# Set-up and first two steps of a conditional attention block in another order

## The chip, the cores and the metric

The kernel runs on one NeuronCore of a Trainium2 chip. The metric is the time of the whole kernel on the device in microseconds (us). Before the change the median of three runs is 350.76 us (348.23, 350.76, 350.86).

## The reference, cut to what matters

Sixteen batches of 256 tokens with 256 features go through one block: a normalisation scaled by a condition, attention with 16 heads of 16 features, a projection with residual, and a second conditional normalisation.

```python
h = _sln(hidden, w, ln_g, ln_b, Wg, bg, Wb, bb)     # gamma(w) * ln(hidden) + beta(w)
qkv = (h @ Wqkv.T + bqkv).reshape(B, N, num_heads, hd, 3)
energy = jnp.einsum('bhqd,bhkd->bhqk', q, k)
att = jax.nn.softmax(energy, axis=-1) / D ** 0.5
out = jnp.einsum('bhqk,bhkd->bhqd', att, v)          # heads put side by side again
h1 = (out @ Wp.T + bp) + hidden
return _sln(h1, w, ln_g, ln_b, Wg, bg, Wb, bb) + h1
```

## The kernel before, in words

**Numbers.** Everything is float32. To multiply on TensorE with enough precision, each operand is split into a high part of type `fp32r` (`hT_h`, `wqkv_h`, `qk_h`) and a low part, the difference (`hT_l`, `wqkv_l`, `qk_l`); a product is three matmuls (high by high, low by high, high by low).

**Stacks.** Per batch, q and k of each head are copied by DMA into `qst` and `kst`, where one head has its high and low parts on different partitions, so that a single contraction gives q times k. A batch has two groups of eight heads (`g` = 0, 1). For each group `send(a, g, t, low)` (L286) on SyncE's queue issues two DMAs of 128 KB: `t` is 0 for q and 1 for k, `low` is 0 for the high part and 1 for the low part. A whole group is eight DMAs. The places of `kst` that no DMA writes must be 1.0 (`ones_k`, L455, GpSimd) and those of `qst` 0 (`clear_q`, ScalarE). The sends of k wait for that fill through `kpad_ready`.

**Two passes of scores.** `scores_max(a, h)` (L1003) computes the scores of head h of batch a into the banks `sa0`, `sa1`; VectorE reduces each bank to row maxima (`maximum`, L681, the TENSOR_REDUCE of L688). After eight heads TensorE transposes the maxima (`transpose_max`, L1067), ScalarE makes the high part `m_h` (`high_max`, L505), VectorE the low part `m_l` (`low_max`, L692), and two small DMAs put both as two more rows into `qst` (`maxima`, L361, GpSimd; for batch 0 group 0 ScalarE issues them itself, L566). Then `scores(b, h)` (L1016) computes the scores less the maximum into `st0`, `st1`, and ScalarE takes the exponential (L602). A `scores_max` may run at most two heads ahead of VectorE's maxima, since there are two banks.

**Steps.** Each engine runs its own program of steps; step b has 16 slots h, one for each head. In slot h of step b TensorE computes `scores(b, h)` and `scores_max(b + 1, h)`, and between them the other work of the neighbouring batches in slots given by constants at L45 to L55: q, k and v projections, `turn_x` (L1092, transposes the normalised input of batch b + 3), `weigh` (weights times v), the output projection. Step -1 has no `scores`: only the maxima of batch 0, the k projection of batch 1 (slots 0 to 3), the v projections of batches 0 and 1 (`V_FIRST`, slots 4 to 6 and 9 to 12) and `turn_x(2)` in slot `X_FIRST` = 8.

**Order on each engine.** Every engine executes its list in order, and semaphores hold it. The order of each list is written out by hand. In step -1 the following matters:
- GpSimd: `low_full(1, 0)` (low part of batch 1's q, L415) in slot 0. In slot 5: `rstd_x(2)`, `low_full(1, 1)` (low part of batch 1's k, which gives `kl_ready` its second count), `norm_x(2)` (xn of batch 2, two instructions of L378), then `wp_l`. In slot 12 `low_h(2)`.
- TensorE, slot 8: `scores_max(0, 8)` and then `turn_x(2)`, which waits for `xn_ready`; slot 9: `scores_max(0, 9)` and `transpose_max(0, 0)`.
- ScalarE, slot `X_FIRST` + 1 = 9: `hT` of batch 2 (L584, waits for `turn_x(2)`) and `hT_h` (L503). Slot 10: `high_max(0, 0)` and the two DMAs of L569, and slot 13 `high_v(1)`.
- VectorE, slot 9: `low_max(0, 0)`, which waits for `high_max(0, 0)`, ahead of `maximum(0, 9)`.
- SyncE's queue: the sends of batch 0 (the high part of k of group 0 goes by ScalarE's queue, `high_k0`, L620), then those of batch 1, in the order that the code below shows.

In step 0, slot 1, TensorE transposes the maxima of heads 8 to 15 of batch 0 (`transpose_max(0, 1)`), ScalarE takes `high_max(0, 1)` in slot 2, VectorE `low_max(0, 1)` in the middle of slot 2, and GpSimd issues `maxima(0, 1)` in slot 3; `scores(0, 8)` waits for these.

Of the kernel before, what the change touches and what calls it, by code (L numbers as in the profile page):

```python
# [32 lines left out]
P = 128  # L33
B, N, D, H = 16, 256, 256, 16
HD = D // H
# [11 lines left out]
S_QH, S_KH, S_VH = 5, 7, 9  # L47
WARM = (10, 4, 4, 4)
V_FIRST = ((4, 5, 6, 6), (9, 10, 11, 12))
X_FIRST = 8  # L50
PIECE = 2
NSTK = 8
NX = 6
# [4 lines left out]
def cond_block(nc, x, condT, vectors, WgT, WbT, WqkvT, WpT, bp, out):  # L58
    gb_dram = nc.dram_tensor("gb_rows", (B, 2 * D), F32, kind="Internal").ap()
    with ExitStack() as ctx:  # L60
# [177 lines left out]
        def has(a):  # L238

            return 0 <= a < B  # L240

        def first(a):

            return a == 0
# [28 lines left out]
        def _(sp):  # L273
# [12 lines left out]
            def send(a, g, t, low):  # L286

                p, s = par(a), stack_in[g][par(a)]
                wait(sp, st_done, 16 * (a - 2) + HH * (g + 1))
                if a < 2 and t == 0:  # L290
                    sp.wait_ge(qpad_ready, 2 * a + g + 1)
                if a < 2 and t == 1:
                    sp.wait_ge(kpad_ready, a + 1)
                wait(sp, ((qh_ready, ql_ready), (kh_ready, kl_ready))[t][low], 1 * a + 1)
                src = (qk_h, qk_l)[low][:, p, t, g, :]
                for n in (low, low + 2) if t == 0 else (2 * low, 2 * low + 1):
                    sp.dma_start(raw((qst, kst)[t][PART_ROW[n]:P:P // HD, p, g * HH:(g + 1) * HH, :]),
                                 raw(src)).then_inc(s, 16)
# [34 lines left out]

            send(0, 0, 0, 0)
            send(0, 0, 0, 1)
            send(0, 0, 1, 1)
            for t in range(2):
                for low in range(2):
                    send(0, 1, t, low)
# [16 lines left out]
        def _(pool):  # L356
# [61 lines left out]
            def step(b):  # L418
                for h in range(H):
                    if h == 5 and has(b):  # L420

                        one, two = has(b + 3), has(b - 2)
                        if one:
                            wait(pool, v_step, 3 * (b + 3) + 3)
                            wait(pool, xn_ready, 1 * (b + 3))
                        if two:
                            wait(pool, ln2_step, 4 * (b - 2) + 3)
                            wait(pool, y_ready, 1 * (b - 2))
                        which = slice(0 if one else 1, 2 if two else 1)
                        pool.tensor_tensor(rstd[:, which], vare[:, which], minus_half[:, which],  # L430
                                           ALU.pow).then_inc(rstd_ready, 1)
                    if first(b + 1) and h == 0:
                        low_full(1, 0, ql_ready)
                    if first(b + 1) and h == 5:
                        rstd_x(2)
                        low_full(1, 1, kl_ready)
                        norm_x(2)
                        pool.wait_ge(wph_ready, 1)
                        pool.tensor_tensor(wp_l[:], wp[:], wp_h[:], ALU.subtract).then_inc(wpl_ready, 1)
                    if h == 3:  # L440
                        maxima(b, 1)
                    if h == 11 and has(b):
                        maxima(b + 1, 0)
                    if h == 6 and has(b - 2):
                        add_beta(b - 2)
                    if h == 5 and has(b + 3) and has(b):
                        norm_x(b + 3)
                    if h == 0 and has(b - 1):
                        add_bias(b - 1)
                    if h in (13, 14) and b == B - 2:  # L450
                        add_bias(b + h - 13)
                    if h == 12:
                        low_h(b + 3)
# [20 lines left out]
                o = pool.tensor_scalar(bias_cols[:, k, :], ones[:, 0:P], vecs[:, 6, k:k + 1], D ** -0.5, ALU.mult, ALU.mult)  # L474
            o.then_inc(bias_cols_ready, 1)
            pool.memset(v_st[:, :, :, :, HD:VC].rearrange("p a t h d -> p (a t h) d"), D ** 0.5).then_inc(v_ones_ready, 1)
            rstd_x(1)
            pool.wait_ge(xn_ready, 2)
            ones_k(1, 0, H).then_inc(kpad_ready, 1)
            pool.wait_ge(wvh_ready, 1)  # L480
            pool.tensor_tensor(wqkv_l[:, :, 2 * D:3 * D], wqkv[:, :, 2 * D:3 * D], wqkv_h[:, :, 2 * D:3 * D],
                               ALU.subtract).then_inc(wvl_ready, 1)
# [13 lines left out]
        def _(act):  # L496
# [55 lines left out]
            def step(b):  # L552
                for h in range(H):
                    if h == S_O1:
                        evict_out(b - 1, 1)
                    if h == S_O0:
                        evict_out(b, 0)
                    if h == S_QH and not first(b + 1):
                        high_q(b + 2)
                    if h == S_KH and not first(b + 1):  # L560
                        high_k(b + 2)
                    if h == S_MT1 + 1 and has(b):
                        high_max(b, 1, pv_ps[0])
                    if h == S_MT0 + 1 and has(b + 1):
                        high_max(b + 1, 0, pv_ps[1] if first(b + 1) else m1)
                    if h == S_MT0 + 1 and first(b + 1):  # L566
                        for r, m, ready in ((0, m_h, mh_ready), (1, m_l, ml_ready)):
                            act.wait_ge(ready, 1)
                            act.dma_start(raw(qst[MAX_ROW + r:MAX_ROW + 1 + r, 0, 0:HH, :])  # L569
                                          .rearrange("a h (t n) -> a (h t) n", t=TT),  # L570
                                          raw(m[:, 0, :])).then_inc(max_first, 16)
                    if h == S_AT + 1 and has(b - 1):
                        wait(act, attT_done, 1 * (b - 1) + 1)
                        wait(act, proj_done, 1 * (b - 2) + 1)
                        nc.scalar.activation(aT_h[:].rearrange("p k n -> p (k n)"), pv_ps[1][:],
                                             ACT.Copy).then_inc(aTh_ready, 1)
                    if h == S_VH and has(b + 1) and has(b - 1):
                        high_v(b + 1, m0)
                    if h == (X_FIRST if first(b + 1) else S_XT) + 1 and has(b + 3):
                        a = b + 3  # L580
                        wait(act, xnT_done, 1 * a + 1)
                        wait(act, hTl_ready, 1 * a)
                        for k in range(KT):
                            o = nc.scalar.activation(hT[:, k, :], m0[:, k * N:(k + 1) * N], ACT.Identity,  # L584
                                                     bias=bfull[:, k, a:a + 1], scale=gfull[:, k, a:a + 1])
                        o.then_inc(hT_ready, 1)
                    if h == (X_FIRST if first(b + 1) else S_XT) + 1:
                        high_h(b + 3)
                    if h == 4 and first(b + 1):
                        high_k(1)  # L590
                        full(1, 1, m1)
                    if h == 7 and first(b + 1):
                        high_v(0, st_ps[0])
                    if h == 13 and first(b + 1):
                        high_v(1, st_ps[1])
                    if has(b):

                        i = 16 * b + h
                        wait(act, st_done, i + 1)
                        if h % HH == 0:  # L600
                            wait(act, pv_done, 2 * (b - 1) + h // HH + 1)
                        nc.scalar.activation(p32[:, h, :], st_ps[h % 2][:], ACT.Exp).then_inc(exp_done, 1)  # L602
# [17 lines left out]
            def high_k0():  # L620

                act.wait_ge(kpad_ready, 1)
                act.wait_ge(kh_ready, 1)
                for r in PART_ROW[0:2]:
                    act.dma_start(raw(kst[r:P:P // HD, 0, 0:HH, :]),
                                  raw(qk_h[:, 0, 1, 0, :])).then_inc(stack_in[0][0], 16)

            def full(a, t, ps):

# [50 lines left out]
        def _(dve):  # L680
# [169 lines left out]
            def step(b):  # L850
# [14 lines left out]
                    (15, 0): [lambda: normalise(b, 0, 0)],  # L865
                    (15, 1): [lambda: normalise(b, 0, 1)],
                }
                if first(b + 1):
                    for slot in ((4, 0), (4, 1), (5, 0), (5, 1), (7, 1), (11, 0)):
                        del between[slot]  # L870
                    between[(9, 0)] = [lambda: low_max(0, 0)]
# [41 lines left out]
            low_qk(0, 0, m0, qh_ready, ql_ready)  # L913
            low_qk(0, 1, m1, kh_ready, kl_ready)
            norm1(1, 3)
            for stage in range(3):
                norm1(2, stage)
            h_direct(1)
            low_h_direct(1)
            set_up_rows()  # L920

            steps(step)
# [44 lines left out]
        def _(pe):  # L967
# [278 lines left out]
            def step(b):  # L1246
                for h in range(H):
# [18 lines left out]
                        out_by_token(b - 1, 1)  # L1266
                    if h == S_OT0:
                        out_by_token(b, 0)
                    if h == S_MT1 and has(b):
                        wait(pe, att_ready, 2 * (b - 1) + 1)  # L1270
                        if first(b):
                            pe.wait_ge(gbrow_ready, 1)
                        transpose_max(b, 1, pv_ps[0])
# [103 lines left out]
```

## Time and profile before

| | |
|---|---|
| runs | 348.23, 350.76, 350.86 us, median 350.76 us |
| profiled execution | 349.5 us on the device; 347.7 us from its first to its last instruction |
| TensorE (PE) busy | 334.0 us, 96% |
| VectorE (DVE) busy | 297.0 us, 85% |
| ScalarE (ACT) busy | 242.8 us, 70% |
| GpSimd (POOL) busy | 159.0 us, 46% |
| mean granted TensorE clock | 0.990 of full speed |

The page cuts the span into 40 equal slices of 8.7 us. A digit is the busy share of a slice in tenths:

```profile
PE   8886989999999999999999999999999999999993
PEclk9997899999999999999999999999999999999999
```

TensorE is nearly always busy except in the first five slices and the last; the clock granted to it is below full speed in the fourth and fifth, from about 26 to 43 us.

### The profile page before, as it was taken

To read this page: it belongs to the slowest core of one execution; us is meant where nothing else is said; L and a number is where in the kernel's file an instruction comes from. 1 tells how busy PE (TensorE), PEld (TensorE's weight loads), DVE (VectorE), ACT (ScalarE), POOL (GpSimd) and SP (SyncE) were. 2 spreads that over 40 slices of the span, in tenths; PEclk is the share of its full clock that TensorE was granted. 3 is DMA by queue.
4 is the path that set the end of the run, shared out by engine and by line. 5 is a ranking of instruction groups with operands and counts; after the bars stand their busy time and mean duration, and the time that the engine had idled before them with its cause. 6 is when DMAs were issued, how large, how long until landed. Compare 5 with 4: busy or idle time off the path is not lost.

```text
span 347.7 us, 8982 instructions
## 1 busy us (share of the span) xinstructions
PE 334.0 (96%) x3173; PEld 288.6 (83%) x3173; DVE 297.0 (85%) x728; ACT 242.8 (70%) x476; POOL 159.0 (46%) x187
## 2 busy tenths in 40 slices
PE   8886989999999999999999999999999999999993
PEld 4675968889898888888898888888898888888773
DVE  4874877789898989989898989989898988998684
ACT  7762686868678686868687686868687686766740
POOL 5476261525464462726454462726454453225330
PEclk9997899999999999999999999999999999999999
DMA  8487245544555465565545565656546454652011
GB/s 239 128 202 204 58 123 151 150 134 129 161 131 158 135 180 155 136 173 139 157 133 156 134 176 153 141 154 160 156 135 154 106 170 124 168 147 75 18 60 60
DMA packets 47705, 48.87 MB, mean 141 GB/s; under 512 B 6287, under 2 KB 41374, under 8 KB 47662
## 3 DMA queue, kind: packets, MB, share of 16 engines
q1 hardware_dynamic: 44782, 47.00, 49.3%
q0 software_dynamic: 1984, 0.51, 0.9%
q10 hardware_dynamic: 896, 0.80, 0.8%
q8 instruction: 25, 0.41, 0.5%
q14 instruction: 18, 0.15, 0.1%
HBM read 9.99 MB, written 4.23 MB: 41 GB/s over the span
## 4 chain that ended last, share of the span: by engine, by line
PE 86%; DVE 5%; ACT 2%; DMA 2%; POOL 2%; issue 2%; SPq 0%; DVEq 0%; POOLq 0%; ACTq 0%
PE m L969 24%; PE st L969 19%; PE sa L969 18%; PE pv L969 17%; PE pv L1058 4%; PE pv L1139 2%; PE m L1098 2%; DMA wqkv<-WqkvT_dram 2%; DVE mx L688 1%; DVE qk_l L723 1%; POOL qk_l L415 1%; POOL xn L378 1%; PE pv L1072 1%; PE m L1072 1%; ACT qk_h L522 0%
## 5 line engine op out<-in xcount | busy, mean ns | idle before, releaser
L688 DVE TENSOR_REDUCE mx<-sa 128x2 f32<-128x512 f32 x256 | 171.6, 683 | 30.1 <-PE sa L969 29.0
L602 ACT ACTIVATE p<-st 128x512 f32<-128x512 f32 x240 | 140.9, 598 | 38.0 <-PE st L969 33.9
L969 PE MATMUL sa<-kst,qst 126*128 126x256 f32 x512 | 106.5, 290 | 1.6 <-DVE mx L688 1.1
L969 PE MATMUL st<-qst,kst 128*128 128x256 f32 x496 | 104.0, 292 | 0.7 <-DMA qst<-m_l 0.5
L969 PEld LDWEIGHTS st<-qst,kst 128*128 128x128 f32 x496 | 75.1, 188 | 14.3 <-issue 12.8
L969 PEld LDWEIGHTS sa<-kst,qst 126*128 126x128 f32 x512 | 80.0, 193 | 3.8 <-DVE mx L688 2.1
L369 POOL DMA_DIRECT2D qst<-m_h x31 | 17.6, 566 | 117.0 <-DVE m_l L697 117.0
L969 PE MATMUL pv<-p,v_st 128*32 128x256 f32 x1008 | 61.0, 382 | 0.0
L969 PEld LDWEIGHTS pv<-p,v_st 128*32 128x32 f32 x1008 | 29.5, 109 | 21.0 <-ACT p L602 1.8
L969 PE MATMUL m<-hT_h,wqkv_h 128*128 128x256 f32 x128 | 36.8, 300 | 1.4 <-issue 0.8
L378 POOL TENSOR_SCALAR xn<-xa,mv,rstd 128x256 f32<-128x256 f32 x28 | 34.2, 1227 | 1.4
L969 PE MATMUL m<-hT_h,wqkv_l 128*128 128x256 f32 x128 | 34.4, 280 | 0.4 <-DVE wqkv_l L909 0.4
L969 PE MATMUL m<-hT_l,wqkv_h 128*128 128x256 f32 x128 | 34.2, 279 | 0.0
L430 POOL TENSOR_TENSOR rstd<-vare,minus_half 128x4 f32<-128x4 f32 (+1 forms) x15 | 14.2, 947 | 40.4 <-DVE vare L745 36.3
L550 ACT ACTIVATE oT<-pv 128x512 f32<-128x512 f32 x29 | 17.2, 594 | 21.6 <-PE pv L969 21.6
L723 DVE SCALAR_TENSOR_TENSOR qk_l<-m,vecs,qk_h 128x256 fp32r<-128x256 f32 x60 | 25.9, 473 | 0.6 <-ACT qk_h L522 0.6
L969 PEld LDWEIGHTS m<-hT_h,wqkv_h 128*128 128x128 f32 x128 | 23.5, 189 | 2.3 <-ACT wqkv_h L642 1.2
L969 PEld LDWEIGHTS m<-hT_h,wqkv_l 128*128 128x128 f32 x128 | 23.6, 190 | 0.6 <-DVE wqkv_l L909 0.6
L969 PEld LDWEIGHTS m<-hT_l,wqkv_h 128*128 128x128 f32 x128 | 23.4, 187 | 0.0
L396 POOL TENSOR_TENSOR h1b<-h,gb 128x512 f32<-128x512 f32 x15 | 19.3, 1289 | 6.9 <-DVE h L784 6.9
L387 POOL TENSOR_TENSOR xa<-xa,bias_b 128x512 f32<-128x512 f32 x16 | 20.6, 1292 | 0.0
L410 POOL TENSOR_TENSOR hT_l<-hT,hT_h 128x512 fp32r<-128x512 f32 x14 | 18.0, 1289 | 4.0 <-ACT hT_h L503 4.0
(149 smaller groups left out, 568.3 us busy)
## 6 DMA issues: line engine op xcount, KB each, us to landing
qst<-qk_h SPq DMA_DIRECT2D x64, 128.0 KB, 2.4
qst<-qk_l SPq DMA_DIRECT2D x64, 128.0 KB, 2.5
kst<-qk_l SPq DMA_DIRECT2D x64, 128.0 KB, 2.7
kst<-qk_h SPq DMA_DIRECT2D x62, 128.0 KB, 2.4
xa<-x_dram SPq DMA_DIRECT2D x16, 256.0 KB, 3.0
gb<-gb_rows SPq DMA_DIRECT2D x16, 256.0 KB, 3.9
out_dram<-y SPq DMA_DIRECT2D x15, 256.0 KB, 3.4
wqkv<-WqkvT_dram SPq DMA_DIRECT2D x1, 512.0 KB, 5.8
```

What stands on the lines that cost most here:

```text
L369: pool.dma_start(raw(qst[MAX_ROW + r:MAX_ROW + 1 + r, p, g * HH:(g + 1) * HH, :]) .rearrange("a h (t n) -> a (h t) n", t=TT), raw(m[:, g, ...
L378: o = pool.tensor_scalar(xn[:, t, :], xbuf(a)[:, t, :], mv[:, t, 0:1], rstd[:, 0, t:t + 1], ALU.subtract, ALU.mult)
L387: pool.tensor_tensor(xbuf(a), xbuf(a), bias_b[:].rearrange("p (a n) -> p a n", a=1).broadcast_to([P, TT, D]), ALU.add).then_inc(xdb_ready, 1)
L396: pool.tensor_tensor(h1b[:], h1[:], gb[:, par(a), D:2 * D].rearrange("p (a n) -> p a n", a=1) .broadcast_to([P, TT, D]), ALU.add).then_inc ...
L410: pool.tensor_tensor(hT_l[:, par(a)], hT[:], hT_h[:, par(a)], ALU.subtract).then_inc(hTl_ready, 1)
L430: pool.tensor_tensor(rstd[:, which], vare[:, which], minus_half[:, which], ALU.pow).then_inc(rstd_ready, 1)
L550: nc.scalar.activation(oT[:, g, :], pv_ps[g][:], ACT.Copy).then_inc(oT_ready, 1)
L602: nc.scalar.activation(p32[:, h, :], st_ps[h % 2][:], ACT.Exp).then_inc(exp_done, 1)
L688: dve.tensor_reduce(mx[:, par(a), h // HH, (h % HH) * TT:(h % HH + 1) * TT], sa_ps[h % 2][:].rearrange("p (t n) -> p t n", t=TT), AX.X, AL ...
L723: o = dve.scalar_tensor_tensor(out=qk_l[:, par(a), t, g, :], in0=ps[:, g * N:(g + 1) * N], scalar=vecs[:, 4 + t, g:g + 1], in1=qk_h[:, par ...
L969: return nc.tensor.matmul(o, l, r, start=start, stop=stop)
L1058: o = nc.tensor.transpose(pv_ps[g][:, t * N + c * P:t * N + (c + 1) * P], oT[:, g, c * N + t * P:c * N + (t + 1) * P], ident[:])
```

## The change

Six edits, all in the set-up and in steps -1 and 0. `X_FIRST` goes from 8 to 10, on TensorE and (one slot later) on ScalarE. On GpSimd xn of batch 2 comes ahead of the low part of batch 1's k, and the fill of batch 1's `kst` is cut in two, the first eight heads ahead of `rstd_x(1)`. The two sends of the low part of k of batch 0, group 0 move from SyncE's queue to ScalarE's. In step 0 the transpose of the second maxima and the `high_max` and `low_max` behind it come one slot sooner. On VectorE the small statistics of batch 2 (`norm1(2, 1)` and `norm1(2, 2)`) come behind `h_direct(1)` and `low_h_direct(1)`.

```diff
-X_FIRST = 8
+X_FIRST = 10
@@ sync: the sends ahead of the steps
             send(0, 0, 0, 0)
             send(0, 0, 0, 1)
-            send(0, 0, 1, 1)
@@ gpsimd, step
                     if first(b + 1) and h == 0:
                         low_full(1, 0, ql_ready)
+                        rstd_x(2)
+                        norm_x(2)
                     if first(b + 1) and h == 5:
-                        rstd_x(2)
                         low_full(1, 1, kl_ready)
-                        norm_x(2)
@@ gpsimd, set-up
+            ones_k(1, 0, HH)
             rstd_x(1)
             pool.wait_ge(xn_ready, 2)
-            ones_k(1, 0, H).then_inc(kpad_ready, 1)
+            ones_k(1, HH, H).then_inc(kpad_ready, 1)
@@ scalar, step
-                    if h == S_MT1 + 1 and has(b):
+                    if h == (0 if first(b) else S_MT1) + 1 and has(b):
                         high_max(b, 1, pv_ps[0])
@@ scalar, high_k0
                 for r in PART_ROW[0:2]:
                     act.dma_start(raw(kst[r:P:P // HD, 0, 0:HH, :]),
                                   raw(qk_h[:, 0, 1, 0, :])).then_inc(stack_in[0][0], 16)
+                act.wait_ge(kl_ready, 1)
+                for r in PART_ROW[2:4]:
+                    act.dma_start(raw(kst[r:P:P // HD, 0, 0:HH, :]),
+                                  raw(qk_l[:, 0, 1, 0, :])).then_inc(stack_in[0][0], 16)
@@ vector, step
+                if first(b):
+                    between[(1, 1)] = between.pop((2, 1))
@@ vector, set-up
             norm1(1, 3)
-            for stage in range(3):
-                norm1(2, stage)
+            norm1(2, 0)
             h_direct(1)
             low_h_direct(1)
+            norm1(2, 1)
+            norm1(2, 2)
             set_up_rows()
@@ tensor, step
-                    if h == S_MT1 and has(b):
+                    if h == (0 if first(b) else S_MT1) and has(b):
                         wait(pe, att_ready, 2 * (b - 1) + 1)
                         if first(b):
                             pe.wait_ge(gbrow_ready, 1)
                         transpose_max(b, 1, pv_ps[0])
```

## Rows read from the trace of the kernel before

**Rows 1.** Windows: start:end, length, busy us per engine, clock, DMA share, GB/s.
```profile
20.00:50.00 30.00, 25.05 (x189) 22.19 (x187) 20.68 (x41) 16.98 (x36) 15.87 (x17) 0.89 0.57 149
50.00:340.00 290.00, 289.32 (x2876) 253.06 (x2876) 259.65 (x633) 211.44 (x423) 130.62 (x143) 1.00 0.51 138
```
**Rows 2.** Chain of waits, first 60 us: start us, us, what it went through.
```profile
25.10 1.30 POOL qk_l L415
26.39 2.43 POOL xn L378 x2
28.96 0.64 PE m L1098 x4
...
44.82 0.80 DVE qk_l L723 x2
...
45.66 0.33 PE m L1072
```
**Rows 3.** Windows, same columns, the stretch at the lower clock.
```profile
30.00:36.60 6.60, 5.55 (x24) 4.95 (x24) 4.06 (x7) 2.03 (x5) 1.33 (x2) 0.50 0.74 190
```
**Rows 4.** Timeline of VectorE, 21 to 40 us; in brackets idle before, and releaser.
```profile
21.21 4.55 DVE L688 TENSOR_REDUCE mx<-sa 128x2 f32<-128x512 f32 x7 [1.52 <-PE sa L969]
26.01 1.29 DVE L688 TENSOR_REDUCE mx<-sa 128x2 f32<-128x512 f32 x2 [0.25 <-PE sa L969]
31.50 0.28 DVE L697 SCALAR_TENSOR_TENSOR m_l<-pv,m_h 16x128 fp32r<-16x128 f32 x1 [4.20 <-ACT m_h L512]
...
33.26 0.69 DVE L688 TENSOR_REDUCE mx<-sa 128x2 f32<-128x512 f32 x1 [0.29 <-PE sa L969]
34.33 0.69 DVE L688 TENSOR_REDUCE mx<-sa 128x2 f32<-128x512 f32 x1 [0.37 <-PE sa L969]
35.39 1.29 DVE L688 TENSOR_REDUCE mx<-sa 128x2 f32<-128x512 f32 x2 [0.38 <-PE sa L969]
36.90 2.01 DVE L688 TENSOR_REDUCE mx<-sa 128x2 f32<-128x512 f32 x3 [0.22 <-PE sa L969]
39.16 0.69 DVE L688 TENSOR_REDUCE mx<-sa 128x2 f32<-128x512 f32 x1 [0.25 <-PE sa L969]
39.76 0.27 DVE L697 SCALAR_TENSOR_TENSOR m_l<-pv,m_h 16x128 fp32r<-16x128 f32 x1
```
**Rows 5.** Chain of waits, first 60 us: TensorE's pieces at full clock.
```profile
37.10 0.24 PE sa L969 x2
37.34 0.36 PE m L969 x3
...
46.76 0.44 PE m L1098 x4
```
**Rows 6.** Timeline of GpSimd: set-up and step -1.
```profile
13.30 0.72 POOL L464 TENSOR_TENSOR rstd<-vare,minus_half 128x2 f32<-128x2 f32 x1 [2.11 <-DVE vare L745]
16.24 3.81 POOL L458 MEMSET kst<- 128x512 f32 x8 [2.22 <-DVE xn L750]
...
23.09 0.71 POOL L464 TENSOR_TENSOR rstd<-vare,minus_half 128x2 f32<-128x2 f32 x1
```
**Rows 7.** Timeline of SyncE's queue: batch 1's last k send of group 0.
```profile
27.82 1.20 SPq L297 DMA_DIRECT2D kst<-qk_l  x2
```
**Rows 8.** Page, DMA issues: count, KB each, median us from issue to landing.
```profile
kst<-qk_l SPq DMA_DIRECT2D x64, 128.0 KB, 2.7
```
**Rows 9.** Timeline of ScalarE and its queue, around the first sends.
```profile
14.71 1.35 ACTq L625 DMA_DIRECT2D kst<-qk_h  x2
17.12 1.25 ACT L616 ACTIVATE hT_h<-st,bfull,gfull 128x256 fp32r<-128x256 f32 x2 [2.49 <-PE st L1098]
```
**Rows 10.** Windows, same columns, while batch 0 is stacked.
```profile
16.00:21.00 5.00, 3.93 (x25) 2.77 (x24) 3.47 (x11) 2.72 (x7) 4.76 (x9) 1.00 1.11 250
```
**Rows 11.** Waits of TensorE, 20 to 50 us: us in total, times, longest.
```profile
PE st L969 <- DMA qst<-m_l: 0.5, 1, 0.5
PE sa L969 <- DMA kst<-qk_l: 0.5, 1, 0.5
```

## The prediction
> **What bounds the kernel now.** I read the windows first. From 50 to 340 us TensorE is busy 289.3 of 290.0 us at full clock; from 20 to 50 us it is busy 25.1 of 30.0 us and its mean granted clock is 0.89 [rows 1]. So whatever moves the moment at which TensorE takes over moves the end by the same amount, and only the front can give anything. The second view, the chain of waits [rows 2], shows what set that moment: GpSimd's low part of batch 1's k (25.10), then xn of batch 2 (26.39, 2.43 us), then `turn_x(2)` at 28.96. TensorE's list is in order, so slot 8 of step -1 stood idle about 2.6 us until xn was there, with `scores_max(0, 9)` behind it. The clock fell behind this idle time: from 30.0 to 36.6 us it is 0.50, the 1.2 GHz level [rows 3].
>
> The third view, VectorE's timeline, gives the bill [rows 4]. The sixteen maxima of batch 0 run from 21.21 on. Behind the ninth, VectorE sits 4.20 us idle: `low_max(0, 0)` stands ahead of `maximum(0, 9)` and waits for ScalarE's `m_h`, which stood behind `hT` and `hT_h` of batch 2, which waited for `turn_x(2)`. Then come gaps of 0.29, 0.37, 0.38, 0.22 and 0.25 us, in which VectorE waits for a half-clocked TensorE. With the 0.25 ahead of the eighth maximum the idle time from 21.21 to 39.16 is 5.96 us. From 39.16 VectorE has no gap up to 45.62, where its low part of batch 2's k releases TensorE (chain: 44.82 + 0.80, then `transpose_max(1, 0)` at 45.66 [rows 2]). From there TensorE is the bound. So 21 to 45.6 us is a VectorE stretch with 5.96 us of holes, and the question is how many holes the change closes.
>
> **xn of batch 2 first, X_FIRST 10.** GpSimd ends `low_full(1, 0)` at about 23.1, its rstd takes 0.71 (from 23.09 [rows 6]), xn 2.43 more [rows 2]: xn is there at 26.2, or 26.5 with the 0.25 us delay worked out below, not at 28.8. TensorE reaches `turn_x(2)` now behind `scores_max(0, 10)`, which waits for the maximum of head 8, at 27.3 (26.01 + 1.29 [rows 4]). So xn has nearly 1 us in hand and the idle 2.6 us goes. On ScalarE `high_max(0, 0)` stands now ahead of `hT`. The maxima of heads 0 to 7 end at 26.65, the transpose takes until about 27.2 (0.3), `m_h` 0.25: `low_max` starts at 27.5, and the 4.20 us hole becomes 0.2. Behind it run heads 9 to 15 at 0.66 us each (4.55 / 7 = 0.65 [rows 4]). TensorE's share per slot is 0.24 for two scores and 0.36 for three projections, 0.60 us [rows 5], just under VectorE's pace. Only slot 10 has 0.44 more for `turn_x` [rows 5], 1.04 in all, which I cost at a gap of 0.25. The maximum of head 15 ends at 27.7 + 7 x 0.66 + 0.25 = 32.6 us. Before, it was the first of the three from 36.90, thus at 37.57.
>
> **The maxima of step 0 one slot sooner.** TensorE now wants the maximum of head 15 in slot 0, ahead of q's first quarter (0.36) and `scores(0, 1)` (0.24), which hid this wait before. Transpose at 32.6, then 0.11 + 0.36 + 0.24, then `scores_max(1, 1)` and its drain (0.5): `maximum(1, 1)` can start at 33.85, while `maximum(1, 0)` ended at 33.25. That is a new hole of 0.6 us on VectorE, the price of this edit. In return `m_l` is ready at 34.75 by this count. Before it was 39.76 + 0.27 = 40.03 [rows 4] and `scores(0, 8)` waited 0.5 us for its landing [rows 11]. TensorE would wait less there, but VectorE sets the pace in that stretch, so I count nothing.
>
> Left of the 5.96 us are 0.25 + 0.2 + 0.25 + 0.65 (the 0.6, rounded up): 1.35. **Saved: 4.6 us** on VectorE; counted through single starts I get 4.5 (`maximum(1, 3)` ends at 36.1, not 40.6). I take 4.5.
>
> **The low part of batch 1's k behind xn.** It ends at about 26.5 + 1.3 = 27.8 us. SyncE's queue sent it at 27.82 before [rows 7], since the queue was then the slower one. Now the queue is 1.3 us ahead by the moved send, and waits for this: all it gained is spent here, and the eight DMAs of group 1 behind it leave when they did (1.3 us for each pair, the last about 34.3). The send lands at about 28.5 + 2.7 [rows 8] = 31.2; `scores_max(1, 0)` wants it at 32.0. Margin 0.8 us, cost nothing; if GpSimd were 1 us later, this wait would be the next bound, us for us. Group 1 is landed by 37 and wanted at about 39.
>
> **k's low rows on ScalarE's queue.** Its two issues of the high part ran 14.71 to 16.06. Two more take as much, 1.35 us, up to 17.4, and `hT_h` of batch 1 started at 17.12 [rows 9]: 0.3 us later. The second half of it had waited for VectorE, which now comes to `h_direct(1)` 0.1 us sooner; net 0.25 us later for `project_second`, for q of batch 1 and so for GpSimd's `low_full(1, 0)` (used above). Does the first score come sooner? It waited 0.5 us for these rows [rows 11]. The DMA engines carry 250 GB/s with a share of 1.11 from 16 to 21 us [rows 10], that is, they have no room, and an earlier issue only changes who waits. Bounds: 0.25 us sooner (the projection ahead of it then sets the start) and 0.6 us later (one more 128 KB transfer at 250 GB/s is 0.5 us, in the same engines). I take 0. The Trainium skill, DMA: Bandwidth & Descriptors, Issuing engines are not separate DMA queues, says that DMAs from all issuers interleave on the same 16 engines and that a second issuer saves only the time to issue. By that rule the move would give 0 and the sum stays; a count by issue time alone would have given 0.25 us.
>
> **GpSimd's fills.** Eight fills take 3.81 us [rows 6]; four of them, 1.9 us, now stand in the 2.11 us that GpSimd idled ahead of rstd [rows 6]. That hides them by 0.2 us; behind rstd there was another idle of 2.22 us, so that a slip costs nothing either. The other four end at 18.15 instead of 20.0, and v's low part starts sooner; nobody waits for it before slot 4. Cost and gain 0. VectorE's `norm1` pieces (0.4 us) move into the idle 1.52 us ahead of the first maximum [rows 4]: 0.
>
> **The sum.** 349.5 (profiled execution) - 4.5 = 345.0 us. This execution lies 1.3 us below the median of the runs, and the mean of all four is 349.8; against that the sum is 345.3. I predict **345.4 us**.
>
> **Rivals.**
> 1. *The clock falls all the same* (0.12). In slots 13 to 15 TensorE has only 0.24 us of work in 0.66 us. Before, the clock fell behind an idle 2.6 us and stayed at 1.2 GHz for 6.6 us although TensorE was busy 5.55 of them [rows 3]. If it falls at about 32 us, the 6.6 us behind it do half their work: 3.3 us back, saving 1.2, 348.6 us. Against it: the shares in these slots are above those of the empty 2.6 us. The Trainium skill, TensorE: Matmul & The Clock Gate, Part 1, has it that the default state is throttled and that activity releases it. The fall behind the idle stretch agrees; by that rule the thin slots are the place to fear.
> 2. *Late landings* (0.15). The first score 0.6 us later and batch 1's first stack 1 us later than I think, both from full DMA engines: saving 4.5 - 0.6 - 0.9 = 3.0, 346.8 us.
> 3. *Given back at the hand-over* (0.06). The gain on VectorE meets something of TensorE's own between 33 and 45 us (it was busy nearly all that time); then only the idle 2.6 us comes off: 347.2 us.
> 4. *Slower* (0.05). SyncE's queue: batch 1's last k send and eight DMAs behind it hang on GpSimd's `low_full(1, 1)`, now behind xn. From 32.0 us each us of lateness is lost at `scores_max(1, 0)`; from 36.5 on the change loses. xn and the low part would have to take 8 us instead of 3.7, or rstd wait for VectorE until 27: priced at 6.5 us late, 345.4 + 6.5 = 351.9, past 354.3 with 9 us. Nothing in the rows points there.
>
> **Chances.** Forecast 0.62. About 1% (3.5 us) is what a measurement of this kernel can tell, so faster means under 347.25 us. From the forecast 0.56 falls there, from rival 2 0.09: faster 0.65. Rivals 1 and 3, half of rival 2 and the forecast's edge: within 1% 0.31. Slower 0.04. The range goes from 343.6 (all holes but 0.25 closed, 5.7 us, from 349.5, less scatter of 0.2) to 348.9 (rival 1 and scatter).
>
> **What would show it.** Right: no wait of `turn_x(2)` for xn; VectorE's wait for `m_h` of batch 0 under 0.5 us; clock 1.00 from 20 to 50 us; `transpose_max(1, 0)` near 41.2; a hole near 0.6 us ahead of `maximum(1, 1)`; the first score at 20.4 to 21.2; from there to the end the same length as before. Wrong: clock 0.50 anywhere from 28 to 40 us; `scores_max(1, 0)` waiting for a `kst` landing; SyncE's queue still sending group 1 after 36 us.

## The result and the profile after

The changed kernel takes 345.31 us (median of four runs, 344.94 to 347.6); the kernel before 349.72 us (median of four, 348.23 to 350.86). The ratio is 0.9898 with a 95% interval of 0.9861 to 0.9935. The profiled execution took 345.56 us, its span is 343.8 us. Predicted were 345.4 us.

First the windows of the kernel after, to be read against [rows 1] (columns as there).

```profile
20.00:50.00 30.00, 27.46 (x218) 23.79 (x217) 25.69 (x50) 20.65 (x43) 16.69 (x17) 1.00 0.59 152
50.00:340.00 290.00, 288.25 (x2866) 252.09 (x2865) 258.97 (x636) 207.90 (x416) 129.76 (x142) 1.00 0.51 139
```

From 20 to 50 us TensorE is busy 27.5 instead of 25.1 us, and the granted clock is 1.00 instead of 0.89. The same stretch that was at 0.50 [rows 3]:

```profile
30.00:36.60 6.60, 6.10 (x45) 5.36 (x44) 5.95 (x11) 4.65 (x10) 2.37 (x3) 1.00 0.72 192
```

VectorE's timeline of the kernel after, which answers to [rows 4] (L692 is `maximum`, L701 `low_max`):

```profile
21.77 4.55 DVE L692 TENSOR_REDUCE mx<-sa 128x2 f32<-128x512 f32 x7 [0.60 <-PE sa L976]
26.56 1.29 DVE L692 TENSOR_REDUCE mx<-sa 128x2 f32<-128x512 f32 x2 [0.24 <-PE sa L976]
28.26 0.28 DVE L701 SCALAR_TENSOR_TENSOR m_l<-pv,m_h 16x128 fp32r<-16x128 f32 x1 [0.41 <-ACT m_h L512]
28.47 5.18 DVE L692 TENSOR_REDUCE mx<-sa 128x2 f32<-128x512 f32 x8
34.31 0.69 DVE L692 TENSOR_REDUCE mx<-sa 128x2 f32<-128x512 f32 x1 [0.66 <-PE sa L976]
34.91 0.27 DVE L701 SCALAR_TENSOR_TENSOR m_l<-pv,m_h 16x128 fp32r<-16x128 f32 x1
```

The hole for `m_h` has gone from 4.20 to 0.41 us. The five small gaps behind it are one of 0.66 us ahead of `maximum(1, 1)`. All holes that the timeline lists are together 0.24 + 0.41 + 0.66 = 1.31 us against 5.96. But the row of seven starts at 21.77, not at 21.21. The chain of waits of the kernel after says why, and gives the hand-over to TensorE:

```profile
16.65 4.53 DMA kst<-qk_l
...
21.23 0.50 PE sa L976 x2
...
40.63 0.80 DVE qk_l L727 x2
...
41.47 0.33 PE m L1079
```

The first score (21.23; 20.66 before) waited for k's low rows, whose last DMA took 4.53 us from its issue on ScalarE's queue to landing. `transpose_max(1, 0)` starts at 41.47 instead of 45.66 [rows 2], 4.19 us sooner; the span is 3.9 us shorter.

**Three segments.** Executions differ by up to 2.8 us before the first stack is sent: the start of k's high part on ScalarE (second `qk_h`) lies between 13.35 and 16.11 us whatever the kernel. Three later segments are free of that, so I compare kernels by them; each is from one profile. A: from that start to the first score on TensorE. B: from there to `transpose_max(1, 0)`, the hand-over. C: from there to the end of the span. The hand-over is taken from the chain of waits, where a piece begins when the one ahead of it has ended. Where TensorE did not stand idle before it (e6, e7, e9, e10, e11), TensorE's timeline has the same start 0.13 to 0.16 us sooner, so B of these five is up to 0.16 us too long beside the others, and C as much too short. The ratio of a row is to executions of the kernel before from the same session (medians 349.72 us for the kernel after, 348.92 for e1 to e4, 349.13 for e5 to e9, 348.71 for e10 and e11).

| kernel | A | B | C | median us | ratio to before |
|---|---|---|---|---|---|
| before | 6.87 | 25.00 | 302.04 | 349.72 | |
| after | 7.52 | 20.24 | 302.33 | 345.31 | 0.9898 (0.9861 to 0.9935) |
| e1_xn_only | 6.72 | 20.04 | 302.07 | 344.41 | 0.9871 (0.9836 to 0.9905) |
| e2_low_on_sync | 6.76 | 20.26 | 302.04 | 344.89 | 0.9896 (0.9853 to 0.9938) |
| e3_max_slot_back | 7.46 | 20.03 | 302.03 | 345.16 | 0.9901 (0.9876 to 0.9927) |
| e4_filled_hole | 6.77 | 23.75 | 302.05 | 348.91 | 1.0000 (0.9975 to 1.0026) |
| e5_xfirst_alone | 6.79 | 21.04 | 302.16 | 345.35 | 0.9888 (0.9825 to 0.9950) |
| e6_pool_alone | 6.77 | 21.59 | 301.99 | 346.22 | 0.9921 (0.9885 to 0.9957) |
| e7_sync_held | 6.80 | 20.78 | 301.77 | 345.20 | 0.9872 (0.9816 to 0.9927) |
| e9_three_back | 6.77 | 20.18 | 301.88 | 344.37 | 0.9855 (0.9800 to 0.9909) |
| e10_stats_early | 6.78 | 20.28 | 301.78 | 344.35 | 0.9861 (0.9835 to 0.9887) |
| e11_stats_and_low_max | 6.73 | 20.32 | 301.94 | 344.37 | 0.9875 (0.9849 to 0.9902) |
| e4_again | 6.79 | 23.75 | 302.05 | one run, 350.55 | |
| before_again | 6.78 | 24.28 | 302.09 | one run, 348.72 | |

Two things can be read before any argument. C is the same within 0.6 us in all (0.4 with the starts of the timeline), so the kernels differ ahead of the hand-over. And A has two values: 7.5 us in the two kernels whose first low rows of k go by ScalarE's queue with SyncE's group 1 beside them, 6.7 to 6.9 in the twelve other profiles.

### The profile page after: what moved, and what is told of

Its sections match the earlier page's. It is cut to its first block, busy times and chain, and to the rows that moved or that the text cites. A ratio compares the mean times of both kernels' runs of the same rounds, so it can differ in the third digit from the quotient of the medians.

```text
span 343.8 us, 8981 instructions
## 1 busy us (share of the span) xinstructions
PE 332.5 (97%) x3173; PEld 286.8 (83%) x3173; DVE 298.3 (87%) x728; ACT 242.8 (71%) x476; POOL 159.1 (46%) x187
## 4 chain that ended last, share of the span: by engine, by line
PE 87%; DVE 5%; DMA 3%; ACT 1%; issue 1%; ACTq 1%; SPq 0%; DVEq 0%
PE m L976 24%; PE st L976 19%; PE sa L976 18%; PE pv L976 17%; PE pv L1065 4%; DVE mx L692 3%; PE pv L1146 2%; PE m L1105 2%; DMA wqkv<-WqkvT_dram 2%; DMA kst<-qk_l 1%; PE pv L1079 1%; PE m L1079 1%; ACT p L602 0%; DVE qk_l L727 0%; ACTq L625 0%
## 5 line engine op out<-in xcount | busy, mean ns | idle before, releaser
L692 DVE TENSOR_REDUCE mx<-sa 128x2 f32<-128x512 f32 x256 | 171.5, 684 | 28.4 <-PE sa L976 27.3
L976 PEld LDWEIGHTS sa<-kst,qst 126*128 126x128 f32 x512 | 78.6, 189 | 4.6 <-DVE mx L692 1.7
L976 PE MATMUL m<-hT_l,wqkv_h 128*128 128x256 f32 x128 | 34.3, 279 | 0.0
L395 POOL TENSOR_TENSOR h1b<-h,gb 128x512 f32<-128x512 f32 x15 | 19.4, 1291 | 6.9 <-DVE h L788 6.9
```

Source lines behind the costliest of these rows:

```text
L395: pool.tensor_tensor(h1b[:], h1[:], gb[:, par(a), D:2 * D].rearrange("p (a n) -> p a n", a=1) .broadcast_to([P, TT, D]), ALU.add).then_inc ...
L692: dve.tensor_reduce(mx[:, par(a), h // HH, (h % HH) * TT:(h % HH + 1) * TT], sa_ps[h % 2][:].rearrange("p (t n) -> p t n", t=TT), AX.X, AL ...
L976: return nc.tensor.matmul(o, l, r, start=start, stop=stop)
```

## The experiments

**e1, the main pair alone.** On the kernel before:

```diff
-X_FIRST = 8
+X_FIRST = 10
@@ gpsimd step, slot 0 of step -1
                         low_full(1, 0, ql_ready)
+                        rstd_x(2)
+                        norm_x(2)
@@ slot 5
-                        rstd_x(2)
                         low_full(1, 1, kl_ready)
-                        norm_x(2)
```

> The kernel before with two edits alone: X_FIRST 10, and rstd_x(2) and norm_x(2) ahead of low_full(1, 1) on GpSimd. Theory: the hand-over to TensorE (start of transpose_max(1, 0)) is the start of the first maximum, plus 18.4 us of VectorE's work, plus its holes: before 21.2 + 18.4 + 6.0 = 45.7, after the whole change 21.8 + 18.4 + 1.3 = 41.5. This kernel keeps the first maximum at 21.2 and has holes of 0.25 and 0.4: hand-over at 40.3, 1.1 us sooner than the whole change; clock 1.00 throughout; about 344.2 us. Rival: the other edits carry a part of the gain (the maxima of step 0, k's low rows), then the hand-over is at 41.5 or later and the time 345.3 us or more.

Measured: 344.41 us, A 6.72, B 20.04. The two edits alone do at least as much as the whole change; the intervals of the two ratios overlap, and it is A that differs clearly. VectorE's holes in B, from its timeline (a third, of 0.25 us, stands ahead of the eighth maximum):

```profile
27.13 0.28 DVE L697 SCALAR_TENSOR_TENSOR m_l<-pv,m_h 16x128 fp32r<-16x128 f32 x1 [0.41 <-ACT m_h L512]
...
33.62 0.69 DVE L688 TENSOR_REDUCE mx<-sa 128x2 f32<-128x512 f32 x1 [0.24 <-PE sa L969]
```

0.25 + 0.41 + 0.24 = 0.9 us. The rival, that the other edits carry a part, falls. But VectorE's work does not set the pace all the way. Between the two holes the chain of waits runs over ScalarE and then TensorE: ScalarE issues the two DMAs of `m_h` (L569), makes `hT` and `hT_h` of batch 2 and then `high_v(1)` (L540), and from 30.64 on TensorE works without a pause until `maximum(1, 1)`:

```profile
27.12 0.57 ACTq L569
...
28.91 0.57 ACT hT L584
...
30.13 0.49 ACT v_st L540
...
30.64 0.51 PE sa L969 x2
...
33.62 0.69 DVE mx L688
```

In the kernel after, the same stretch of the chain is VectorE's maxima.

**e2, k's low rows back on SyncE's queue.** The whole change without one edit:

```diff
             send(0, 0, 0, 1)
+            send(0, 0, 1, 1)
@@ scalar, high_k0
-                act.wait_ge(kl_ready, 1)
-                for r in PART_ROW[2:4]:
-                    act.dma_start(raw(kst[r:P:P // HD, 0, 0:HH, :]),
-                                  raw(qk_l[:, 0, 1, 0, :])).then_inc(stack_in[0][0], 16)
```

> The whole change with one edit undone: the low part of k of batch 0, group 0 is sent by SyncE's queue again, behind q's. Theory: the move costs, since two issuers crowd DMA engines that are full; the first maximum comes back from 21.77 to 21.2 and the hand-over from 41.5 to 40.9, about 344.8 us. Rival: the late landing has another cause (the transfers of that execution), and the first maximum stays at 21.8 or goes later, 345.3 us or more.

Measured: A 6.76 instead of 7.52, B unchanged (20.26 against 20.24), 344.89 us. The chain of waits has the last DMA landing sooner although it was issued later:

```profile
17.35 3.40 DMA kst<-qk_l
```

So the move costs 0.7 us, as the theory had it; the difference of the medians, 0.4 us, is within their intervals and proves nothing by itself.

**e3, the maxima of step 0 back in slot 1.** The whole change without `(0 if first(b) else S_MT1)` in the two places and without `between.pop`.

> The whole change with one edit undone: transpose, high part and low part of the second maxima of batch 0 stand in step 0 where they stood before. Theory: the hole of 0.66 us ahead of maximum(1, 1) closes and the hand-over comes at 40.8 instead of 41.5, about 344.7 us; TensorE waits about 0.4 us for the landing of m_l at scores(0, 8), beside VectorE's work, which costs nothing. Rival: that wait is on the path and takes back what the hole gives, hand-over 41.3 to 41.5, 345.3 us.

Measured: B 20.03 instead of 20.24; the last gap on VectorE is 0.25 instead of 0.66 us; TensorE waits 0.7 us at `scores(0, 8)`. Median 345.16 us, no measurable difference to 345.31. The direction is as expected, but of the 0.4 us of the hole only half comes back: the chain of e3 runs over ScalarE and TensorE up to `maximum(1, 1)`, as in e1.

**e4, the idle time filled.** On the kernel before:

```diff
                             pe.wait_ge(full_ready, 1)
+                        if first(b + 1):
+                            pe.wait_ge(gbrow_ready, 1)
+                            for _ in range(FILL):          # FILL = 10
+                                mm(pv_ps[0][:], zeros[:, 0:P], zeros[:], True, True)
                         turn_x(b + 3)
```

> The kernel before with ten matmuls of zeros (2.1 us) put in front of turn_x(2), in the 2.6 us for which TensorE stood idle. Theory: the clock fell because of that idle time; it stays at 1.00, the hole of 4.20 us stays, and of the 1.51 us of holes behind it about 1.2 go: hand-over 44.4, about 1.2 us less than the kernel before. Rival: the clock falls for another reason (the thin slots) and nothing moves.

B is 23.75 us, 1.25 less than in the first profile of before. The clock stays at 1.00 from 20 to 50 us, the big hole stays, the five small ones behind it, 1.51 us in before, shrink to one of 0.25; that is 1.26 us less, and B lost 1.25. The theory holds in the profile, and the rival falls:

```profile
31.06 0.28 DVE L698 SCALAR_TENSOR_TENSOR m_l<-pv,m_h 16x128 fp32r<-16x128 f32 x1 [4.13 <-ACT m_h L513]
31.27 6.03 DVE L689 TENSOR_REDUCE mx<-sa 128x2 f32<-128x512 f32 x9
```

But the median did not move (348.91 us, ratio 1.0000). The times lay in groups of 347.95 to 348.4 and 349.4 to 350.4 us, and each of the two kernels has a second profile.

> The kernel before with the ten matmuls of zeros in the idle 2.6 us, once more, for a second profile: its times fell into two groups (347.95 to 348.4 and 349.4 to 350.4 us). Theory: the difference is the granted clock, which fell all the same in some executions; a profile of the slower group shows 0.50 between 28 and 40 us, and one of the faster group 1.00 and 23.75 us from the first score to the hand-over. Rival: the difference lies ahead of the first score (the start of k's high part moves, 13.4 to 16.1 us in the profiles so far).

> The kernel before once more, for a second profile: its times lie between 347.9 and 349.4 us with some at 351, and the profile shown is of 349.5 us. Theory: 25.0 us from the first score to the hand-over, with the clock at 0.50 for some 6.8 us behind the idle 2.6 us; the scatter of its times is that of the set-up. Rival: the clock falls in some executions only, which would put the hand-over at 23.8 us where it does not.

The second profile of e4, of 350.55 us, has B 23.75 again at clock 1.00, against its theory; it is slower since k's high part starts at 16.11 and not at 13.53, as its rival had it. The second profile of before has B 24.28, between its theory (25.0) and its rival (23.8). Two of its windows:

```profile
29.00:31.00 2.00, 2.00 (x11) 2.00 (x11) 0.00 (x0) 1.03 (x3) 0.92 (x1) 0.50 0.73 198
...
32.00:34.00 2.00, 1.47 (x12) 1.26 (x10) 2.00 (x5) 0.00 (x0) 0.97 (x1) 0.99 0.75 204
```

Here the clock was down to 1.2 GHz only until about 32 us, not until 36.6. The three values of B order themselves by it: never down 23.75, down until 32 us 24.28, down until 36.6 us 25.00. So of the gain in B (25.00 - 20.04 = 4.96 us, e1) the clock was 1.25 us in one execution of before and 0.53 in the other. The rest, 23.75 - 20.04 = 3.71 us, is the hole for `m_h`, 4.13 us in e4 and 0.41 in e1.

Why e4's median does not show this can be read in part from the spans, which are on record for every execution. From the first to the last instruction e4 took 346.45 us in the median of ten, and before 347.1 us in the median of 19 of the same session, 0.65 us more. What lies outside the span is 1.75 to 1.88 us in every execution of every other kernel, but 1.93 to 3.26 us in six of e4's ten; that hides the gain in its times. Where this extra time comes from is open.

**e5 and e6, each of the main pair alone.** e5 has only `X_FIRST = 10`, e6 only GpSimd's order.

> The kernel before with X_FIRST 10 alone; GpSimd keeps its order. Time from the first score to the hand-over: 25.0 us before, 20.0 with both edits. Theory: VectorE's hole for m_h goes from 4.2 to 0.4, since high_max(0, 0) no longer stands behind hT of batch 2; TensorE wants turn_x(2) at about 28.3 and gets xn at 28.8, an idle 0.7 us that costs VectorE some 0.3 and leaves the clock at 1.00: 20.4 us, 344.7 us in all. So this one constant carries nearly all of the gain, and GpSimd's order 0.4 us of it. Rival: xn is the root (the chain of waits names it), and without GpSimd's order 2 us or more of the gain stay out: 22 us or more, 347 us.

> The kernel before with GpSimd's order alone (rstd_x(2), norm_x(2) ahead of low_full(1, 1)); X_FIRST stays 8. Theory: TensorE gets xn at 26.2 and idles 0.4 instead of 2.6 us, the clock stays at 1.00; but m_h still stands behind hT and hT_h on ScalarE, so that VectorE keeps a hole of 1.8 us in place of 4.2, and the small gaps behind it go: first score to hand-over 21.5 us against 25.0, about 345.6 us. Rival: if xn were the whole cause, 20.0 us as with both edits, 344.2 us.

e5: B 21.04 (345.35 us). The constant alone gives 4.0 of the 5.0 us, and the rival (22 or more) falls. I had expected 20.4: xn is late by 0.98 us, and VectorE pays 1.02 for it, not 0.3. VectorE's timeline:

```profile
29.93 4.76 DVE L688 TENSOR_REDUCE mx<-sa 128x2 f32<-128x512 f32 x7 [1.02 <-PE sa L969]
```

e6: B 21.59 (346.22 us), expected 21.5, so the rival (20.0) falls. TensorE waits only 0.2 us for xn, yet VectorE still has this hole, since `m_h` stands behind `hT` and `hT_h` on ScalarE:

```profile
28.80 0.28 DVE L697 SCALAR_TENSOR_TENSOR m_l<-pv,m_h 16x128 fp32r<-16x128 f32 x1 [1.85 <-ACT m_h L512]
```

The chain of waits named xn as the cause [rows 2]. GpSimd's order alone takes 3.4 of the 5.0 us off B: the hole for `m_h` goes from 4.20 to 1.85 us, and the small gaps of the low clock go. The rest of the hole, 1.85 to 0.41 us, is the order of two pieces on ScalarE. The two gains overlap: the constant is worth 4.0 us alone and 1.6 behind GpSimd's order, and GpSimd's order 3.4 us alone and 1.0 behind the constant.

**e7, SyncE's queue held.** The whole change, and SyncE waits for `hTh_ready` 2 ahead of group 1:

```diff
             send(0, 0, 0, 1)
+            sp.wait_ge(hTh_ready, 2)
```

> The whole change, with SyncE's queue held until hT_h of batch 1 is done (about 18.5 us) before it sends group 1 of batch 0. From the start of k's high part to the first score: 6.7 to 6.9 us in the four kernels that send k's low rows from SyncE's queue, 7.5 in the two that send them from ScalarE's. Theory: the low rows land late since group 1, 1.3 us ahead, shares the full DMA engines with them; held back, they land by 20 us and the first score comes 6.7 us behind k's high part, 0.7 us less in all, if group 1 still lands by 26.3. Rival: four transfers in a row on ScalarE's queue are slow by themselves; then it stays at 7.5.

A falls to 6.80 us with four transfers in a row on ScalarE's queue. So these are not slow by themselves; group 1's transfers beside them are what made the rows late, and the rival falls. But B grows to 20.78. Group 1 now lands at 25.85 us and `scores_max(0, 8)` waits 0.34 us for it, which costs about 0.1; the rest is a wait that no theory had. TensorE's timeline:

```profile
39.71 0.50 PE L977 MATMUL st<-qst,kst 128*128 128x256 f32 x2 [1.08 <-DVE mx L693]
```

This is `scores(0, 8)`. VectorE is named since a maximum happened to end just then, but in the program `scores(0, 8)` waits for no maximum, only for an exponential (done at 38.2) and for the landing of the second pair of maxima rows. GpSimd issued `m_l` at 35.28, and its landing took 4.4 us, until 39.7.

**e9, four edits of the change kept and two undone.** X_FIRST, xn, the split fill and VectorE's order of the statistics stay.

> The whole change without the move to ScalarE's queue and without the sooner maxima of step 0; left are X_FIRST 10, GpSimd's order of xn, the split fill and VectorE's order of the statistics. Theory: the two undone edits cost 0.7 and 0.2 to 0.5 us, the fill and the statistics are worth nothing: the same as X_FIRST and xn alone, 6.7 to 6.8 us to the first score, 20.0 us from there to the hand-over, 344.3 us. Rival: the fill and the order of the statistics are worth something and it comes out over 0.3 us faster than those two edits alone.

344.37 us, A 6.77, B 20.18: the same as e1 within 0.15 us. The fill and the statistics are worth nothing. e1 and e9 have the lower medians, 0.9 us under the kernel after. The intervals of the ratios overlap, so the runs alone do not show it; the profiles do, with A and B together 26.76 (e1) and 26.95 us (e9) against 27.76.

**e10 and e11, how far VectorE's work is the bound.** Both start from e1.

```diff
@@ vector, set-up (e10, e11)
             set_up_rows()
+            norm1(3, 0)
@@ vector, step: slot 4, first half, not in step 0 (e10, e11)
-                    (4, 0): [lambda: residual(b - 2, 2), lambda: norm1(b + 3, 0)],
+                    (4, 0): [lambda: residual(b - 2, 2)] + ([] if first(b) else [lambda: norm1(b + 3, 0)]),
@@ vector, step -1 (e11 alone)
-                    between[(9, 0)] = [lambda: low_max(0, 0)]
+                    between[(9, 1)] = [lambda: low_max(0, 0)]
```

> X_FIRST and xn alone (20.04 us from the first score to the hand-over, 344.4 us), and norm1(3, 0), two BATCH_NORM_STATS2 of 0.66 us together, taken off VectorE's list in slot 4 of step 0 and put into its idle 1.4 us ahead of the first maximum. Theory: VectorE has no hole from the ninth maximum to the hand-over but 0.65 us, so its work is the bound and most of 0.66 us comes off, until the next chain binds: m_l of heads 8 to 15 lands 0.64 us late for scores(0, 8) at 38.74, and from there TensorE's own four scores and the transpose reach 39.95, only 0.2 us ahead of the hand-over at 40.13. So 0.2 us are gained, 19.8 us. Rival: the landing is beside the path also now, and all of 0.66 us comes off: 19.4 us, 343.75 us.

> The same, and low_max(0, 0) stands behind maximum(0, 9) on VectorE instead of ahead of it, so that the hole of 0.4 us for m_h is filled with a maximum. ScalarE issues m_h's DMA until 27.7, so m_l may come 0.27 us later without cost. Theory: 0.4 us more off, and the second m_l goes 0.4 us sooner too, so the chain over its landing gives way by as much: 19.4 us from the first score to the hand-over, 343.8 us. Rival: scores(0, 0) then waits for the landing of the first m_l (issued at 27.75, 2.4 us), and nothing is gained over the last kernel: 19.8 us.

B 20.28 and 20.32: no gain from taking 0.66 us of work off VectorE, nor from filling the hole of 0.41. I had expected 19.8 and 19.4. The mechanism named for e10 was there, but stronger, and e10's rival (19.4) falls. Filling the hole could give little, since in e1 the chain leaves VectorE at that place (see e1). The chain of waits of e10, and of e11:

```profile
38.12 3.53 DMA qst<-m_l
...
41.69 0.50 PE st L970 x2
```

```profile
36.02 3.58 DMA qst<-m_l
```

In both the path now goes over GpSimd's DMA of the second `m_l`, and VectorE waits 0.30 and 0.35 us for TensorE's scores just before the hand-over. In e6 and e9 that DMA is on the chain too (3.42 and 3.45 us). In e1 the path goes over VectorE, but the landing (3.1 us) is late as well: TensorE waited 0.64 us at `scores(0, 8)`. So in e1 and e9 two chains end together, and a further gain needs both.

## Why the prediction was right

- *The hand-over sets the end.* C is 302.04 before and 302.33 after; between all kernels 301.77 to 302.33. So the gain ahead of it stayed.
- *xn first, X_FIRST 10.* This was the mechanism, and e1, e5 and e6 show it. xn ended at 26.36 (predicted 26.5) and TensorE did not wait for it. The hole for `m_h` is 0.41 (predicted 0.2), the gap for slot 10 did not show (predicted 0.25). That is 0.04 us off in the sum. One reading was too broad: of the five small gaps of before, which were put down to the half clock, the one of 0.25 us at 39.16 stands at full clock (it was 1.00 again from 37 us on) and is still there in e1 and e4.
- *The maxima of step 0 sooner.* The hole is 0.66 us (predicted 0.6), and the wait of 0.5 us at `scores(0, 8)` is gone. I counted the landing at nothing since VectorE set the pace. It is nearer the path than I wrote: e3 gives back 0.2 instead of 0.4 us, and e6, e7, e9, e10 and e11 have it on the path; in e2, with this edit in, TensorE waits 0.51 us for it. The edit trades one for the other and costs about 0.2 us.
- *k's low part behind xn.* The queue's rows that answer to [rows 7], the last send of group 0 and of group 1, are where I put them: 27.67 (predicted 27.8), and the last pair from 33.09 to 34.29 (predicted 34.3).
- *k's low rows on ScalarE's queue.* This is the term that was mis-sized: taken as 0 with bounds of 0.25 sooner and 0.6 later, it is 0.7 us later (A 7.52 and 7.46 against 6.76), just outside the bound. ScalarE's delay was as counted (`hT_h` of batch 1 at 17.37 instead of 17.12 [rows 9]); the landing was not. The Trainium skill, DMA: Bandwidth & Descriptors, Issuing engines are not separate DMA queues, has the transfers of all issuers interleave on the same engines. e7 agrees: without the interleaved group the rows land in time. A count by that rule gives 0 for bandwidth. What the prediction left out is that group 1 went into the same engines 1.4 us sooner (its first send at 16.43 instead of 17.83), beside the rows that were wanted first.
- *GpSimd's fills.* The four early ones lie from 11.21 to 13.14 us, ahead of rstd at 13.24, and cost nothing (e9 against e1).
- *The sum.* Predicted were 4.5 us off the profiled execution; measured are 349.5 - 345.56 = 3.94, of the span 3.9: B 4.76 less, A 0.65 more, C 0.29 more, the start of k's high part 0.08 sooner. The median moved by 4.4 us, but that it agrees with 4.5 to 0.1 is luck: the two profiles of before alone differ by 0.7 us in B, the 5.96 us were read from the one with the longer fall of the clock, and the cost of the move to ScalarE's queue was left at nothing. The prediction's 345.4 is nearer to 345.31 than its working deserves.
- *Rivals.* The clock did not fall in slots 13 to 15; it was 1.00 in B in every profile without the idle 2.6 us. The view shows TensorE busy for 1.67 us of the 2 us from 31 to 33. It counts each matmul to its end, and so more than the prediction's 0.24 in 0.66 us. The Trainium skill, TensorE: Matmul & The Clock Gate, Part 1, says that activity releases the throttle. e4 agrees: matmuls of zeros in the idle stretch kept 1.00. Of the late landings one came (the first), the other not. At the hand-over nothing was given back that stands out from the scatter of C (0.29 us longer, where all kernels lie within 0.56).

## What to carry to other kernels

When the chain of waits names a late input, look at what stands behind it on every in-order engine. Here the earlier input alone gave 3.4 of 5.0 us, and one constant alone, which put the piece that VectorE waited for ahead of the late one on ScalarE, gave 4.0. Before moving a transfer to a second queue because the first is busy, look whether the DMA engines are full. They were here (share 1.11 [rows 10]), and the move let a transfer that nobody needed yet run beside one that was waited for. Undo the edits of a bundle one by one: six edits gained 4.4 us here, and two of them alone had the median 0.9 us lower still. Read more than one profile of the kernel before: two of the same kernel differed by 0.7 us in the stretch that the change is about.

## What the runs showed of the hardware

- The same kernel, with the same idle 2.58 us of TensorE, had the clock at 1.2 GHz until 32 us in one execution and until 36.6 us in another, and paid 0.53 or 1.25 us for it (against e4).
- The clock can fall without such an idle stretch. In three of the fourteen profiles (the second of before, e2 and e11) it also fell to 0.50 in the set-up, from about 8.1 to 8.7 us on until about 11.5 to 12 us. TensorE had been busy for all or nearly all of the time from 6 us on (transposes, and matmuls with 16 columns). In the other eleven it stayed at 1.00 there.
- A 128 KB transfer inside SBUF took 4.53 and 4.48 us from issue to landing on ScalarE's queue with SyncE's queue sending group 1 beside it (after, e3), and 3.37 to 3.42 us as the last DMA of the group on SyncE's own queue (e1, e2, e9, e10, e11).
- The small DMA of `m_l` that GpSimd issues (8 KB) took 2.1 to 2.3 us from issue to landing for the second maxima of batch 0 in three profiles (after and both of e4), 3.0 to 3.2 in five (both of before, e1, e3, e5), and 3.4 to 4.4 us in six (e6, e9, e10, e11, e2, e7). What lengthens it was not tried and is open.
